# Adding the attention output bias to the first head's folded weights on PE, once, instead of to every tile on POOL

## The chip, the core and the metric

The kernel runs on one core of one Trainium2 chip. The metric is the device time of one execution in microseconds, given as the median of several runs. TensorE is written PE, VectorE DVE, ScalarE ACT, GpSimd POOL and the queue that issues most of the transfers SP, as in the profile.

## What is computed

A cross-attention block followed by a mixture-of-experts block, both with a layer norm ahead of them and a residual sum behind them. `x` is 4 x 1024 x 256, the context 4 x 64 x 192; there are 16 heads of 64 columns and 64 keys.

```
def attention(x, context, Wq, Wk, Wv, Wo, bo):
    q = (x @ Wq)          # heads of 64
    k, v = context @ Wk, context @ Wv
    attn = softmax(q k^T * scale)          # over the 64 keys of a head
    return (attn v over all heads) @ Wo + bo
x = x + attention(layernorm(x), ctx, Wq, Wk, Wv, Wo, bo)
x = x + ffn(layernorm(x))    # shared expert, and the best 2 of 8 experts by a gate
```

## The kernel before

The 4096 rows of x are 32 tiles of 128 rows. The kernel has three stages one behind the other: a preparation, the attention over the 32 tiles, and the expert stage over 103 tiles (20 and 12 shared ones around 71 routed ones), with the routing arithmetic between the last two.

**Preparation.** For every batch b two matrices are folded: `A` (Wq with the keys, so that scores = xn A) and `U` (the values with Wo, so that output = prob U). `U[b, j]` has 128 rows, which are the 64 keys of head 2j and the 64 keys of head 2j+1, and 256 columns. Every operand is split into a high and a low part in the fp32r type, and a product is three matmuls (high by high, low by high, high by low), written by the helper `product` (line 1086, the matmul is line 1092). The order is fixed by the list `plan` (line 379): entries C, W, K, A and then, for j = 0 to 7, V (j+1) and two U entries (j, i), each of which makes two batches. V of number 0 stands ahead of the two last A entries, and V of number 1 ahead of the first U entry. A V entry is a product with 128 and one with 64 contraction rows (192 in all), so six matmuls; a U entry is twelve matmuls of 256 columns with 128 contraction rows. Each entry goes through three engines: PE fills one of eight PSUM banks, ACT copies it out as the high part (line 710, `leave`), DVE subtracts that to get the low part (lines 913 to 933). Weights pass through ACT too (`high`, line 718) and then POOL, which makes their low parts (line 579) and increments `pre_w_lo`; PE waits for that count ahead of each K, V and U entry. In the ACT program the weights for V and U number j+1 are converted at the start of the V entry j.

**The passage to attention.** Every engine waits until all of the preparation is through PE, ACT and DVE (`pre_pe`, `pre_act`, `pre_dve`, all at NPRE). POOL then writes some constants (lines 586 to 596). ACT also waits for `const_ok` at 6, which is a matter of the very start of the kernel, since POOL's first six constants include `yrow` set to zero (line 535, 128 x 1024). ACT later issues DMAs that write these zeros to the accumulators in DRAM (`zero_rows`, line 760).

**Attention.** It is software-pipelined by hand: in step s each engine handles tile s + 1, s, s - 1 and so on, in a fixed order. For a tile: POOL and ACT make the normalized rows `xn`; PE transposes them (line 1165); ACT and DVE make the high and low parts `xTh` and `xTl` (lines 685, 875); PE computes scores (twelve matmuls of 512 columns in L1092); DVE takes maxima (line 862), scales them (`nmax`, line 865), subtracts (line 867); ACT takes exponentials (lines 700, 704); DVE sums and inverts (lines 841, 844); POOL normalizes `prob` (line 566); PE transposes it (line 1175), and multiplies with U (24 matmuls of 256 columns) into bank 5; DVE adds `xres`, the tile of x (line 891), and computes statistics for the second layer norm. SP loads `xres` (line 424). POOL adds `bo_bc`, the bias spread over 128 partitions, to `xres` at line 572, behind its normalization of another tile, and DVE waits for `xb_ok` that this sets. In steps 3, 4 and 5 POOL also makes low parts of the shared expert's weights (lines 601, 603, 606) at the end of its step.

Of the kernel before, what the change touches and what calls it, by code (L numbers as in the profile page):

```python
# [5 lines left out]
F32 = mybir.dt.float32  # L6
# [20 lines left out]
def xattn_moe(nc, x, ctx, Wq, Wk, Wv, Wo, bo, gate_w, gate_b, w1, b1, w3, b3, w2, b2,  # L27
# [43 lines left out]
    with stack:  # L71
# [18 lines left out]
        vTh = sb("vTh", [P, 2, B, 2, NK], F32R, pre)  # L90
        vTl = sb("vTl", [P, 2, B, 2, NK], F32R, pre)
        pre.close()
        xrow = sb("xrow", [P, RING, D], F32)
# [31 lines left out]
        Ul = sb("Ul", [P, B, NJ, D], F32R, att)  # L125
        bo_bc = sb("bo_bc", [P, D], F32, att)

# [105 lines left out]
        wo_in = sem("wo_in")  # L233
        small_in = sem("small_in")
        sw_in = sem("sw_in")
        id_ok = sem("id_ok")
# [39 lines left out]
        O_ok = sem("O_ok")  # L276
        xb_ok = sem("xb_ok")
        x2_ok = sem("x2_ok")
# [128 lines left out]
        def _(sp):  # L407
# [26 lines left out]
            sp.dma_start(wo_raw[:, :, :], Wo.rearrange("(j p) d -> p j d", p=P)).then_inc(wo_in, 16)  # L434
            sp.dma_start(bo_bc[:, :], bo.rearrange("(a d) -> a d", a=1).to_broadcast([P, D])).then_inc(small_in, 16)
            sp.dma_start(gateb_bc[:, :], gate_b.rearrange("(a d) -> a d", a=1).to_broadcast([P, E])).then_inc(small_in, 16)
# [85 lines left out]
        def _(pool):  # L522
# [11 lines left out]
            pool.iota(slots[:, :, 0], pattern=[[0, NU]], base=T, channel_multiplier=1).then_inc(const_ok, 1)  # L534
            pool.memset(yrow[:, :, :], 0.0).then_inc(const_ok, 1)
            pool.wait_ge(const_ok, 6)
            pool.dma_start(slots_dram.rearrange("(p n) c -> p n c", p=P), slots[:, :, :]).then_inc(table_out, 16)
            def tile_step(s, par):
# [23 lines left out]
                if has(t, NT):  # L562
# [4 lines left out]
                                       ALU.mult).then_inc(norm_ok, 1)  # L567
                t = s - 3
                if has(t, NT):
                    p = (par + 1) % 2  # L570
                    wait(pool, xres_in[p], before(t) + 16)
                    pool.tensor_tensor(xres[:, p, :], xres[:, p, :], bo_bc[:, :], ALU.add).then_inc(xb_ok, 1)

            for s in (-1, 0):
                tile_step(s, s % 2)
            for c, (kind, j) in enumerate(w_plan):
                pool.wait_ge(pre_w_hi, c + 1)
                for low, raw, high in zip(*(w_pieces(kind, j, name) for name in ("low", "raw", "high"))):
                    last = pool.tensor_tensor(low, raw, f32(high), ALU.subtract)
                last.then_inc(pre_w_lo, 1)  # L580
            pool.wait_ge(small_in, 96)
            pool.wait_ge(pre_pe, NPRE)
            pool.wait_ge(pre_act, NPRE)
            pool.wait_ge(pre_dve, NPRE)

            pool.memset(ones[:, :], 1.0).then_inc(const_ok, 1)
            pool.memset(tri[:, :], 1.0).then_inc(const_ok, 1)
# [69 lines left out]
        def _(act):  # L657
# [63 lines left out]
            for c, (kind, j, i) in enumerate(plan):  # L721
# [18 lines left out]
                elif kind == "A":  # L740
# [3 lines left out]
                    last.then_inc(pre_act, 1)  # L744
                elif kind == "V":
                    high("V", j + 1)
                    high("O", j + 1)
                    if j == 0:
                        act.wait_ge(vT_zero, 2)
                    for half, r in halves:  # L750
                        last = leave(c, vTh[half, j % 2, :, r, :],
                                     ps[half, c % 8, 0:BK].rearrange("p (b n) -> p b n", b=B))
                    last.then_inc(pre_act, 1)
                else:
                    leave(c, Uh[:, 2 * i:2 * i + 2, j, :], bank.rearrange("p (b d) -> p b d", b=2)).then_inc(pre_act, 1)
            act.wait_ge(pre_pe, NPRE)
            act.wait_ge(pre_dve, NPRE)
            act.wait_ge(small_in, 96)
            def zero_rows(rows):
# [13 lines left out]

            act.wait_ge(const_ok, 6)
            steps(NT, 1, 6, begin_step, begun=0)
# [56 lines left out]
        def _(dve):  # L832
# [3 lines left out]
            def tile_step(s, par):  # L836
# [48 lines left out]
                if has(t, NT):  # L885
                    p = par
                    wait(dve, O_ok, t + 1)
                    wait(dve, xb_ok, t + 1)
                    wait(dve, x2_out[p], before(t))
# [141 lines left out]
            for k, mark in enumerate((first, second)):  # L1031
                link(dve.tensor_tensor(mA[:, :, :], mark[:, :, :], score[:, :, :], ALU.mult))
                link(dve.tensor_reduce(record[:, :, k, 1].bitcast(F32), mA[:, :, :], AX.X, ALU.add))
            dve.wait_ge(small_in, 96)
            unit_step(0, 0)
# [47 lines left out]
        def _(pe):  # L1083
            PARTS = ((0, 0), (1, 0), (0, 1))

            def product(out, stationary, moving, n):


                last = None
                for k in range(n):  # L1090
                    for i, (a, b) in enumerate(PARTS):
                        last = pe.matmul(out, stationary(k, a), moving(k, b), start=(k == 0 and i == 0),  # L1092
                                         stop=(k == n - 1 and i == len(PARTS) - 1))
                return last
# [3 lines left out]
            for c, (kind, j, i) in enumerate(plan):  # L1098
# [23 lines left out]
                else:  # L1122
                    pe.wait_ge(pre_w_lo, w_number["O", j] + 1)
                    pe.wait_ge(pre_dve, number["V", j, 0] + 1)
                    for b in range(2):
                        last = product(bank[:, b * D:(b + 1) * D],
                                       lambda _, part: (vTh, vTl)[part][:, j % 2, 2 * i + b, :, :].rearrange("p a n -> p (a n)"),
                                       lambda _, part: (woh, wol)[part][:, j, :], 1)
                last.then_inc(pre_pe, 1)
            pe.wait_ge(pre_act, NPRE)  # L1130
            pe.wait_ge(pre_dve, NPRE)
            pe.wait_ge(small_in, 96)

# [169 lines left out]
```

## Time and profile before

| What | us |
|---|---|
| median of 3 runs | 806.48 (805.17 to 807.34) |
| the profiled execution | 811.39 |
| its span, first to last instruction | 809.5 |
| preparation, from the span's start | 0 to about 62 |
| attention | about 62 to 319 |
| routing arithmetic, and the last piece of weight loading | about 319 to 430 |
| expert stage | about 330 to 809 |

The profiled execution is 4.9 us longer than the median, and 1.9 us of it lies outside its span. The rows that follow are of its span. A timeline row gives start and duration in us, then engine, line, operation and tiles, and how many instructions it merges; "idle before" is the time that the engine stood still ahead of it, with what released it. A matmul's duration includes its pipeline depth, so that the distance between starts, and not the duration, is what a matmul adds to a stream of them.

### The profile page before, as it was taken

How to read it: one execution, taken by the hardware profiler on the slowest of the kernel's cores; microseconds unless marked ns; L12 is line 12 of the kernel's file. 1: busy time of each engine (PE TensorE's matmuls, PEld its weight loads, DVE VectorE, ACT ScalarE, POOL GpSimd, SP SyncE). 2: the span in 40 equal slices, each digit the busy share in tenths (PEclk: the TensorE clock that was granted, in tenths of full speed). 3: DMA queues.
4: the chain of work that ended last, by engine and by line, in shares of the span. 5: the costliest groups of instructions: out<-in, count | busy, mean ns of one | idle time of the engine just before them, and what ended most of it. 6: DMA issues, size and time to landing. Idle time of an engine off the chain costs nothing.

```text
span 809.5 us, 16280 instructions
## 1 busy us (share of the span) xinstructions
PE 675.1 (83%) x4635; PEld 633.8 (78%) x4636; DVE 535.4 (66%) x1053; ACT 396.9 (49%) x1287; POOL 423.1 (52%) x532
## 2 busy tenths in 40 slices
PE   3996899999999996603007888999999999999995
PEld 2785799999999985602007878999999999999994
DVE  3884888888888874810008888666666666666678
ACT  3995777787778772301007322343444434434432
POOL 4353866556556643377750120667667777676300
PEclk9997999999999999765558999999999999999998
DMA  9202333222222212990002321344444444445595
GB/s 214 80 1 104 129 126 88 77 66 79 66 75 71 66 56 85 296 335 11 1 4 82 106 80 53 60 79 72 72 71 72 77 69 73 73 83 109 88 370 227
DMA packets 65005, 79.96 MB, mean 99 GB/s; under 512 B 11337, under 2 KB 57906, under 8 KB 64946
## 3 DMA queue, kind: packets, MB, share of 16 engines
q1 hardware_dynamic: 47618, 55.81, 22.7%
q0 software_dynamic: 15744, 18.84, 14.7%
q10 hardware_dynamic: 1584, 4.59, 1.5%
q8 instruction: 30, 0.49, 0.2%
q14 instruction: 29, 0.24, 0.1%
HBM read 49.97 MB, written 29.24 MB: 98 GB/s over the span
## 4 chain that ended last, share of the span: by engine, by line
PE 74%; another core or an unknown queue 9%; DVE 8%; issue 3%; DMA 3%; ACT 2%; POOL 1%; SPq 0%; ACTq 0%; DVEq 0%; POOLq 0%
PE ps L1092 62%; PE ps L1247 4%; PE ps L1175 3%; PE ps L1239 2%; PE ps L1152 1%; DMA wq_sb<-in_L_xattn_Wq 1%; DMA xrow<-xn_scratch,slots 1%; DVE w13l L992 1%; DVE uv L969 1%; PE ps L1194 1%; PE ps L1165 1%; DVE hTl L956 1%; DVE hmax L862 0%; DVE w2l L995 0%
## 5 line engine op out<-in xcount | busy, mean ns | idle before, releaser
L641 POOL DMA_INDIRECT acc_scratch<-yrow,slots x71 | 111.5, 1570 | 87.6 <-ACT yrow L802 84.0
L634 POOL DMA_INDIRECT xrow<-xn_scratch,slots x71 | 70.8, 997 | 74.3 <-PE ps L1239 54.5
L802 ACT ACTIVATE yrow<-ps,slots 128x256 f32<-128x256 f32 x71 | 33.7, 474 | 148.1 <-PE ps L1092 148.1
L812 ACT ACTIVATE uxTh<-ps 128x256 fp32r<-128x256 f32 x103 | 38.9, 378 | 133.7 <-remote 71.9
L1092 PE MATMUL ps<-w13h,uxTh 128*128 x284 | 97.5, 343 | 0.0
L1092 PE MATMUL ps<-ws2h,hTh 128*128 128x256 f32 x96 | 29.4, 306 | 78.9 <-DVE hTl L956 55.0
L969 DVE TENSOR_TENSOR uv<-ps,b 128x704 f32<-128x704 f32 x71 | 63.3, 891 | 47.5 <-PE ps L1092 46.8
L1092 PE MATMUL ps<-w13l,uxTh 128*128 x284 | 91.7, 323 | 0.0
L1092 PE MATMUL ps<-w13h,uxTl 128*128 x284 | 91.3, 321 | 0.0
L1092 PEld LDWEIGHTS ps<-ws2h,hTh 128*128 128x128 f32 x96 | 19.0, 197 | 83.7 <-DVE hTl L956 59.5
L625 POOL DMA_INDIRECT slots_scratch<-record,slot x64 | 62.0, 969 | 33.8 <-issue 19.2
L700 ACT ACTIVATE prob<-ps,nmax 128x64 f32<-128x64 f32 x256 | 76.3, 338 | 3.1 <-DVE nmax L865 3.1
L951 DVE TENSOR_TENSOR uxTl<-ps,uxTh 128x256 fp32r<-128x256 f32 x103 | 43.6, 423 | 48.0 <-ACT uxTh L812 43.9
L1092 PE MATMUL ps<-Uh,pTh 128*128 128x256 f32 x256 | 74.9, 293 | 0.0
L1092 PE MATMUL ps<-Uh,pTl 128*128 128x256 f32 x256 | 72.3, 282 | 0.0
L1092 PE MATMUL ps<-Ul,pTh 128*128 128x256 f32 x256 | 71.9, 281 | 0.0
L566 POOL TENSOR_TENSOR prob<-prob,hinv 128x1024 f32<-128x1024 f32 x32 | 61.0, 1905 | 13.0 <-DVE hinv L844 13.0
L1092 PE MATMUL ps<-Ah,xTh 128*128 128x512 f32 x128 | 57.2, 447 | 8.1 <-DVE xTl L875 8.1
L1092 PE MATMUL ps<-w2h,hTh 128*128 x213 | 63.0, 296 | 0.0
L956 DVE TENSOR_TENSOR hTl<-ps,hTh 128x384 fp32r<-128x384 f32 x103 | 57.3, 556 | 7.5 <-issue 7.4
L969 DVE TENSOR_TENSOR uv<-ps,bs 128x704 f32<-128x704 f32 x32 | 28.4, 889 | 50.8 <-remote 31.8
L1092 PE MATMUL ps<-w2l,hTh 128*128 x213 | 60.1, 282 | 0.0
(206 smaller groups left out, 2250.7 us busy)
## 6 DMA issues: line engine op xcount, KB each, us to landing
sums<-acc_scratch SPq DMA_DIRECT2D x16, 512.0 KB, 10.0
w_raw<-in_L_ffn_w SPq DMA_DIRECT2D x16, 352.0 KB
xin<-in_x SPq DMA_DIRECT2D x32, 128.0 KB, 2.5
acc_scratch<-yrow ACTq DMA_DIRECT2D x8, 512.0 KB, 2.7
xres<-in_x SPq DMA_DIRECT2D x32, 128.0 KB, 2.4
acc_scratch<-x SPq DMA_DIRECT2D x32, 128.0 KB, 1.9
xn_scratch<-xn SPq DMA_DIRECT2D x32, 128.0 KB, 2.4
xrow<-xn_scratch SPq DMA_DIRECT2D x32, 128.0 KB
```

Of the source, the lines that this page charges most:

```text
L566: pool.tensor_tensor(heads, heads, hinv[:, p, :].unsqueeze(2).to_broadcast([P, HEADS, NK]), ALU.mult).then_inc(norm_ok, 1)
L625: pool.indirect_dma_start(slots_dram, bass.IndirectOffsetOnAxis(ap=slot[:, k, t:t + 1], axis=0), record[:, t, k, :], None).then_inc(scat_o ...
L634: pool.indirect_dma_start(xrow[:, m, :], None, xn2_dram, bass.IndirectOffsetOnAxis(ap=slots[:, u, 0:1], axis=0)).then_inc(gather_in[m], 16)
L641: pool.indirect_dma_start(acc_dram[u % 2], bass.IndirectOffsetOnAxis(ap=slots[:, u, 0:1], axis=0), yrow[:, m % YRING, :], None, compute_op ...
L700: act.activation(prob[:, p, h * NK:(h + 1) * NK], ps[:, s_bank(p) + h // 8, h % 8 * NK:(h % 8 + 1) * NK], ACT.Exp, bias=nmax[:, p, h - HS: ...
L802: act.activation(yrow[:, y, :], ps[:, 6 + m % 2, 0:D], ACT.Copy, scale=slots[:, bass.ds(u, 1), 1].bitcast(F32)).then_inc(y_ok, 1)
L812: act.activation(uxTh[:, p, :], ps[:, 0, 0:D], ACT.Copy).then_inc(uxTh_ok, 1)
L951: dve.tensor_tensor(uxTl[:, p, :], ps[:, 0, 0:D], f32(uxTh[:, p, :]), ALU.subtract).then_inc(uxTl_ok, 1)
L956: dve.tensor_tensor(hTl[:, :], ps[:, 5, 0:H3], f32(hTh[:, :]), ALU.subtract).then_inc(hTl_ok, 1)
L969: dve.tensor_tensor(uv[:, :, :], ps[:, 1 + 2 * p:3 + 2 * p, 0:H], bias, ALU.add).then_inc(bias_ok, 1)
L1092: last = pe.matmul(out, stationary(k, a), moving(k, b), start=(k == 0 and i == 0), stop=(k == n - 1 and i == len(PARTS) - 1))
L1247: last = pe.transpose(ps[:, 5, k * P:(k + 1) * P], hid[:, p, k * P:(k + 1) * P], ident[:, :])
```

## The change

The bias is no longer spread over 128 partitions but loaded as one row (`bo_row`, 1 x 256), split by ACT and POOL into `boh` and `bol`. Since the probabilities of a head sum to one, adding the bias to each of the 64 rows of U that belong to head 0 adds it once to each row of the output. So the four U products with j = 0 (one for each batch) are not closed after their three matmuls; two more with one contraction row follow, whose stationary operand `head0` is a row with ones in its first 64 of 128 columns and whose moving operands are `boh` and `bol`. POOL's addition at line 572, `bo_bc` and `xb_ok` go; DVE waits for the transfer of `xres` itself.

The five small buffers lie where `yrow` lies. So POOL can set `yrow` to zero only after the preparation: the memset is moved from the start of the kernel to the head of POOL's constants behind the preparation, and ACT, which waited for `const_ok` ahead of its first attention step, waits there for `zero_ok`, which the moved memset sets. `small_in` counts one transfer less.

```diff
@@ sync
-            sp.dma_start(bo_bc[:, :], bo.rearrange("(a d) -> a d", a=1).to_broadcast([P, D])).then_inc(small_in, 16)
+            sp.dma_start(bo_row[0:1, :], bo.rearrange("(a d) -> a d", a=1)).then_inc(bo_in, 16)
@@ gpsimd
-            pool.memset(yrow[:, :, :], 0.0).then_inc(const_ok, 1)
+            pool.memset(head0_raw[0:1, :], 0.0).then_inc(const_ok, 1)
             pool.wait_ge(const_ok, 6)
+            pool.memset(head0_raw[0:1, 0:NK], 1.0).then_inc(head0_ok, 1)
...
-                t = s - 3
-                if has(t, NT):
-                    p = (par + 1) % 2
-                    wait(pool, xres_in[p], before(t) + 16)
-                    pool.tensor_tensor(xres[:, p, :], xres[:, p, :], bo_bc[:, :], ALU.add).then_inc(xb_ok, 1)
...
             for c, (kind, j) in enumerate(w_plan):
+                if (kind, j) == ("V", 1):
+                    pool.wait_ge(bo_hi, 1)
+                    pool.tensor_tensor(bol[0:1, :], bo_row[0:1, :], f32(boh[0:1, :]), ALU.subtract).then_inc(bo_lo, 1)
                 pool.wait_ge(pre_w_hi, c + 1)
...
+            pool.memset(yrow[:, :, :], 0.0).then_inc(zero_ok, 1)
             pool.memset(ones[:, :], 1.0).then_inc(const_ok, 1)
@@ scalar
                 elif kind == "V":
+                    if j == 0:
+                        act.wait_ge(bo_in, 16)
+                        act.wait_ge(head0_ok, 1)
+                        act.activation(head0[0:1, :], head0_raw[0:1, :], ACT.Copy)
+                        act.activation(boh[0:1, :], bo_row[0:1, :], ACT.Copy).then_inc(bo_hi, 1)
                     high("V", j + 1)
                     high("O", j + 1)
...
-            act.wait_ge(const_ok, 6)
+            act.wait_ge(zero_ok, 1)
             steps(NT, 1, 6, begin_step, begun=0)
@@ vector
                     wait(dve, O_ok, t + 1)
-                    wait(dve, xb_ok, t + 1)
+                    wait(dve, xres_in[p], before(t) + 16)
@@ tensor
-            def product(out, stationary, moving, n):
+            def product(out, stationary, moving, n, more=False):
...
-                                         stop=(k == n - 1 and i == len(PARTS) - 1))
+                                         stop=(k == n - 1 and i == len(PARTS) - 1 and not more))
...
-                                       lambda _, part: (woh, wol)[part][:, j, :], 1)
+                                       lambda _, part: (woh, wol)[part][:, j, :], 1, more=j == 0)
+                        if j == 0:
+                            pe.wait_ge(bo_lo, 1)
+                            pe.matmul(bank[:, b * D:(b + 1) * D], head0[0:1, :], boh[0:1, :], start=False, stop=False)
+                            last = pe.matmul(bank[:, b * D:(b + 1) * D], head0[0:1, :], bol[0:1, :], start=False, stop=True)
```

## Rows read from the trace of the kernel before

**Rows 1.** The page's first part: busy time, share and instructions of each engine.
```profile
PE 675.1 (83%) x4635; PEld 633.8 (78%) x4636; DVE 535.4 (66%) x1053; ACT 396.9 (49%) x1287; POOL 423.1 (52%) x532
```

**Rows 2.** Stretches: busy time of PE, PEld, DVE, ACT, POOL; PE clock, DMA, GB/s.
```profile
38.00:61.70 23.70, 22.24 (x152) 19.25 (x151) 20.70 (x42) 21.60 (x62) 11.47 (x22) 1.00 0.00 1
...
61.70:90.00 28.30, 19.97 (x76) 15.61 (x77) 16.04 (x33) 16.99 (x66) 12.44 (x25) 0.82 0.31 107
...
119.00:200.00 81.00, 81.00 (x570) 74.84 (x570) 66.97 (x155) 62.54 (x253) 49.24 (x88) 1.00 0.27 78
```

**Rows 3.** Waits of PE from 0 to 170 us: total, times, longest.
```profile
PE ps L1092 <- DVE xTl L875: 8.1, 4, 2.7
...
PE ps L1165 <- ACT Uh L710: 1.5, 1, 1.5
```

**Rows 4.** Timeline of PE in a V entry of the preparation and the U entry behind it.
```profile
46.08 0.28 PE L1092 MATMUL ps<-ctxTl,wvh 128*128 128x256 f32 x1
46.29 0.38 PE L1092 MATMUL ps<-ctxTh,wvh 64*128 64x256 f32 x1
46.52 0.28 PE L1092 MATMUL ps<-ctxTh,wvl 64*128 64x256 f32 x1
46.63 0.28 PE L1092 MATMUL ps<-ctxTl,wvh 64*128 64x256 f32 x1
46.84 0.38 PE L1092 MATMUL ps<-woh,vTh 128*128 128x256 f32 x1
47.06 0.28 PE L1092 MATMUL ps<-woh,vTl 128*128 128x256 f32 x1
```

**Rows 5.** Timelines of ACT, POOL and PE where V number 1's weights are made.
```profile
39.14 0.51 ACT L718 ACTIVATE wvh<-wv_raw 128x128 fp32r<-128x128 f32 x2
39.54 0.42 ACT L718 ACTIVATE woh<-wo_raw 128x256 fp32r<-128x256 f32 x1
39.84 0.77 ACT L710 ACTIVATE vTh<-ps 64x256 fp32r<-64x256 f32 x2
...
39.72 0.88 POOL L579 TENSOR_TENSOR wvl<-wv_raw,wvh 128x128 fp32r<-128x128 f32 x2 [1.26 <-ACT wvh L718]
40.56 0.73 POOL L579 TENSOR_TENSOR wol<-wo_raw,woh 128x256 fp32r<-128x256 f32 x1
...
40.76 0.30 PE L1092 MATMUL ps<-ctxTh,wvh 128*128 128x256 f32 x1
```

**Rows 6.** The old bias transfer: issue duration in ns and start, time to landing.
```profile
L435 SPq DMA_DIRECT2D bo_bc<-in_L_xattn_bo x1: 6462/6462/6462, 5.7 to 5.7; - x1
...
DMA to landing us min/median/max: 14.3/14.3/14.3
```

**Rows 7.** Timeline: the memset of yrow, and the passage to attention.
```profile
3.27 0.94 POOL L535 MEMSET yrow<- 128x1024 f32 x1
...
61.92 0.60 ACT L678 ACTIVATE xn<-xin,nm,rs 128x256 f32<-128x256 f32 x1 [0.81 <-DVE Ul L932]
61.98 0.20 POOL L586 MEMSET ones<- 128x128 bf16 x1 [5.75 <-DVE Ul L932]
...
62.43 0.36 ACT L685 ACTIVATE xTh<-ps 128x256 fp32r<-128x256 f32 x1
```

**Rows 8.** The chain that ended last: scores of the first and the fourth tile.
```profile
63.30 4.63 PE ps L1092 x12
...
85.81 3.02 PE ps L1092 x12
```

**Rows 9.** POOL and DVE in the ramp; nmax (L865) over all tiles (min/median/max ns).
```profile
82.45 0.72 POOL L572 TENSOR_TENSOR xres<-xres,bo_bc 128x256 f32<-128x256 f32 x1
83.14 1.67 POOL L601 TENSOR_TENSOR ws13l<-ws,ws13h 128x704 fp32r<-128x704 f32 x1
...
83.36 1.47 DVE L865 TENSOR_SCALAR nmax<-hmax 128x8 f32<-128x8 f32 x1
...
L865 DVE TENSOR_SCALAR nmax<-hmax x32: 171/255/1473, 69.2 to 297.1; 128x8 f32<-128x8 f32 x32
```

More of the change, by code:

```diff
@@ L91, in xattn_moe @@
         vTl = sb("vTl", [P, 2, B, 2, NK], F32R, pre)
+        bo_row = sb("bo_row", [P, D], F32, pre)
+        boh = sb("boh", [P, D], F32R, pre)
+        bol = sb("bol", [P, D], F32R, pre)
+        head0_raw = sb("head0_raw", [P, P], F32, pre)
+        head0 = sb("head0", [P, P], F32R, pre)
         pre.close()
@@ L125, in xattn_moe @@
         Ul = sb("Ul", [P, B, NJ, D], F32R, att)
-        bo_bc = sb("bo_bc", [P, D], F32, att)
         xin = sb("xin", [P, 2, D], F32, att)
@@ L234, in xattn_moe @@
         small_in = sem("small_in")
+        bo_in = sem("bo_in")
+        bo_hi = sem("bo_hi")
+        bo_lo = sem("bo_lo")
+        head0_ok = sem("head0_ok")
+        zero_ok = sem("zero_ok")
         sw_in = sem("sw_in")
@@ L276, in xattn_moe @@
         O_ok = sem("O_ok")
-        xb_ok = sem("xb_ok")
         x2_ok = sem("x2_ok")
@@ L580, in _ @@
                 last.then_inc(pre_w_lo, 1)
-            pool.wait_ge(small_in, 96)
+            pool.wait_ge(small_in, 80)
             pool.wait_ge(pre_pe, NPRE)
@@ L757, in _ @@
             act.wait_ge(pre_dve, NPRE)
-            act.wait_ge(small_in, 96)
+            act.wait_ge(small_in, 80)
             def zero_rows(rows):
@@ L1033, in _ @@
                 link(dve.tensor_reduce(record[:, :, k, 1].bitcast(F32), mA[:, :, :], AX.X, ALU.add))
-            dve.wait_ge(small_in, 96)
+            dve.wait_ge(small_in, 80)
             unit_step(0, 0)
@@ L1131, in _ @@
             pe.wait_ge(pre_dve, NPRE)
-            pe.wait_ge(small_in, 96)
+            pe.wait_ge(small_in, 80)
             def tile_step(s, par):
```

## The prediction

> **What bounds the kernel now.** Start with the busy shares: PE is the busiest engine, POOL is busy for half of the span [rows 1]. That says nothing yet of what a microsecond of POOL is worth, so read the stretches [rows 2]. From 119 to 200 us, in the steady part of attention, PE is busy for 81.00 of 81.00 us at full clock, while POOL is busy for 49.24: PE is the bound and has no gap that a shorter POOL could close. In the second half of the preparation (38 to 61.7 us) PE is busy for 22.24 of 23.70 us, also at full clock, and ACT is close behind with 21.60. From 61.7 to 90 us, the ramp of the attention pipeline, PE is busy for only 19.97 of 28.30 us and its mean clock is 0.82: here a chain through all engines sets the pace. The waits of PE say which: four waits for `xTl` make 8.1 us, and 1.5 us passed between preparation and attention [rows 3]. So I read three places: the preparation, where PE is the bound; the passage; and the ramp. The change touches each.
>
> **Removed: 32 additions on POOL.** One takes 0.72 us [rows 9], 23 us in all. In the steady part they lie beside a PE without a gap, and are worth nothing. What hides them is PE's own stream; DVE, the reader of `xres`, waits for the U product behind it. The one place where such an addition stands on the chain is in the ramp: in step 3 it runs from 82.45, the 704-column subtraction for `ws13l` follows it at 83.14 and ends at 84.81, and DVE's `nmax`, started at 83.36, ends only at 84.83, 1.47 us long where its shortest is 0.17 [rows 9]. A DVE instruction of this kind evidently waits until the POOL instruction in progress is through. Behind it in DVE's order comes the `xTl` for which PE waits until 85.81 [rows 3, 8]. Without the addition the subtraction starts and ends 0.69 us sooner (83.14 less 82.45), and DVE and PE with it: a gain of 0.69. Steps 4 and 5 have the same pattern, but PE has work by then, so nothing.
>
> By the Trainium skill (the page SBUF — State Buffer, on what contends on the engine side) a GpSimd instruction and a VectorE instruction that uses two ports exclude each other for their whole length. The row agrees with that: `nmax` ends 0.02 us after the subtraction.
>
> **Added to PE.** Eight matmuls of 256 columns. Their distance within a stream is 0.12 us (46.52 to 46.63) [rows 4], so 8 times 0.118 gives 0.94. But they have one contraction row, and their neighbours 128. The trace has no such matmul; the nearest are those of 64 rows. The first of them starts 0.21 after its predecessor and its successor 0.23 after it; on the way back the distances are 0.21 and 0.22 (46.08, 46.29, 46.52; 46.63, 46.84, 47.06) [rows 4]. Against 0.118 that is 0.09, 0.11, 0.09 and 0.10: one excursion to fewer rows and back costs 0.4 us. The change makes four excursions, one for each batch: 1.6 us. Bounds: nothing if one row costs no switch (0), and twice the excursion if a narrower one costs more (3.2). I take 1.6, the only row that shows a change of rows. PE is the bound there, so this counts in full: 2.5 us.
>
> The Trainium skill (TensorEngine Tiling (Array Packing), key properties) states that a change of tiling mode drains the engine, which would put a price on each change as the rows do; the matmul page (TensorE: Matmul & The Clock Gate, why this matters for your kernels) has a small-row matmul as long as a full one, which taken alone gives the sum without the excursions. That case is a rival below.
>
> **Added to ACT and POOL in the preparation.** ACT copies `head0` (128 columns) and `boh` (256) ahead of the weights of V number 1. By starts, two copies of 128 columns take 0.40 (39.14 to 39.54) and one of 256 takes 0.30 (39.54 to 39.84) [rows 5]: 0.20 and 0.30, 0.5 together. So `boh` starts at 39.34 and ends about 39.75, and the V weights are high at 40.15 in place of 39.65. POOL starts 0.07 behind ACT; its 256-column subtraction is 0.73, at 39.82 to 40.55, and then the two subtractions for V take 0.88, to 41.4 in place of 40.60. PE took up V number 1 at 40.76 [rows 5], only 0.16 behind POOL's end, so it now waits until about 41.5: 0.7 us of stall, on the bound. The bounds are 0.3 (if the small copies cost half of it, with the subtraction of one row shorter) and 0.9. Behind it nothing more is late: the U products wait for `bo_lo` at 40.55, which is past; PE is now behind ACT by more than before, so later weights are in time. The stall and the 2.5 us arrive together at the end of the preparation, because ACT's last copies wait for PE, not the other way round.
>
> The transfer is one row in place of 128 KB. The old one was issued at 5.7 and landed 14.3 us later, about 20 us [rows 6]; ACT needs the row at 39.1. Nothing waits; SP's queue behind it only gets shorter, and what it loads there is used in attention. Two tiny memsets replace a 0.94 us one at POOL's start, where transfers of the weights are what PE waits for: nothing.
>
> **Moved: the memset of yrow.** It takes 0.94 us [rows 7]. POOL can begin it at 61.98, where it now begins `ones`. ACT waits for it before its first attention step: with 0.07 for the semaphore it starts at 62.99 in place of 61.92. Queued behind that wait are `xn` of tile 1 and then `xTh` of tile 0 (62.43), which DVE and PE wait for with the first scores at 63.30 [rows 7, 8]. Nothing covers it: 1.07 us. POOL's constants and its first statistics are late by 0.94 too, but ACT's use of them had room of its own behind the scores of tile 0.
>
> **Sum.** Preparation 0.94 + 1.6 + 0.7 = 3.2; passage 1.07; ramp -0.69: together +3.6 us. The profiled execution has 811.39, so the change would make it 815.0; on the median, 806.48 + 3.6 = 810.1, which is 0.45% slower. About 0.3%, 2.4 us, is what a measurement here can tell from no change.
>
> **Rivals.**
> *The rows cost no switch.* Then PE gets 0.94 and not 2.5: +2.0, 808.5, inside the limit. For it: one row is not 64, and I have one pattern only. Against it: that pattern repeats in each V entry.
> *The clock.* Scores of a tile in the ramp took 4.63 us where the fourth took 3.02 [rows 8], and the mean clock of the ramp was 0.82 [rows 2], so most of the first three groups ran at the lower of the two levels, 1.2 GHz; PE had stood idle ahead of each. The change makes the idle time ahead of the first group a microsecond longer and puts a stall into the preparation. If another group falls to the lower level, that costs 1.6 (4.63 less 3.02), and the result is 811.7.
> *On the other side: the ramp recovers its clock.* If the shift and the shorter gap in step 3 let the groups run at the upper level, each gives back 1.6. From the third group on the sum turns negative: 3.6 - 4.8 = -1.2, 805.3; with no cost for the switches, -2.8, which alone would be measurably faster (803.7). Two groups give 806.9. Against it: the gaps ahead of the first three groups become no shorter.
> *The relief counts after all.* `nmax` has a median of 0.255 where its shortest is 0.171 [rows 9], so POOL's instructions hold it up in most tiles, by 0.08 times 32, 2.7 us. If DVE paced the steady part, the net would be +0.9, 807.4. Against it: PE busy for 81.00 of 81.00 us.
> *The change does not do what it says.* If the new zeroing lay under other work, +2.5, 809.0. I see no such cover.
>
> **How the numbers follow.** The forecast, with its sizes about right: 0.55, 808.9 to 811.0. No switch cost: 0.15. Clock worse: 0.12. Clock better by one or more groups: 0.10, of which 0.03 is measurably faster. The relief: 0.03. The zeroing hidden: 0.05. The range that leaves out some 0.2, half of the clock cases and the ends of the switch's price: 807.2 to 812.0. Slower by over 0.3% (above 808.9) is 0.67: the forecast 0.52, the worse clock 0.12, and 0.03 of the hidden zeroing. Within 0.3% is 0.30, faster 0.03.
>
> **What would show it.** In the profile after: the eight matmuls with starts 0.2 apart at their edges, not 0.12; PE idle for 0.7 ahead of V number 1, released by POOL; a `yrow` memset of 0.94 between the last `Ul` and ACT's first `xn`, and first scores some 4.3 us later than 63.30; `nmax` of step 3 ending 0.69 sooner against the scores ahead of it; a steady step unchanged. It would be wrong if the four U products take 0.12 per matmul throughout, if PE waits somewhere new in the steady part, or if the clock in the ramp differs from 0.82.

## The result, and the profile after

The changed kernel takes 813.87 us (median of 7, 809.54 to 815.85) where the kernel before, measured beside it, takes 805.77 (805.01 to 807.97): a ratio of 1.0093, 95% interval 1.0069 to 1.0118. Measured a second time, beside the kernel before again (a1, below), it was 1.0085 (1.0070 to 1.0100). The change costs 7 to 8 us. The forecast was 3.6, with a range that ended at 812.0.

The profiled execution took 814.34, its span is 812.6. The page of the changed kernel, clock and shares:

```profile
PE 683.1 (84%) x4643; PEld 639.2 (79%) x4644; DVE 533.4 (66%) x1053; ACT 397.8 (49%) x1289; POOL 402.2 (50%) x503
...
PEclk9987899999999999675557999999999999999998
```

Two things differ from [rows 1] and its page: POOL lost 21 us of work, and the clock row begins 99878 where that of the kernel before begins 99979. The 7 in the fourth slice is the passage to attention in both. New are the 8 in the third slice, 41 to 61 us from the start, which is the preparation, and the 8 in the fifth, at the scores of tiles 2 and 3. PE is busy for 8 us more, although only eight small matmuls were added.

The first profile of the kernel before is not a typical one. The weights for Wq landed late in it: PE took up the first weight product at 14.62 us. In a second profile of the same kernel (b1, below) that is 11.53, and 11.67 in the changed kernel. In the other seventeen profiles of this document it lies between 11.50 and 12.36. So the two first profiles, 811.39 and 814.34, are only 3 apart, and stages are compared here by their own lengths, not by the time from the start.

Timeline of PE around the first U products of the changed kernel (L1144 and L1145 are the new matmuls, L1105 is the line of `product`):

```profile
37.81 0.36 PE L1105 MATMUL ps<-ctxTh,wvh 128*128 128x256 f32 x1 [0.56 <-issue]
...
39.23 0.28 PE L1105 MATMUL ps<-wol,vTh 128*128 128x256 f32 x1
39.44 0.38 PE L1144 MATMUL ps<-boh,head 1*128 1x256 f32 x1
39.66 0.28 PE L1145 MATMUL ps<-bol,head 1*128 1x256 f32 x1
39.87 0.38 PE L1105 MATMUL ps<-woh,vTh 128*128 128x256 f32 x1
40.09 0.28 PE L1105 MATMUL ps<-woh,vTl 128*128 128x256 f32 x1
...
45.43 0.41 PE L1105 MATMUL ps<-woh,vTl 128*128 128x256 f32 x1
45.65 0.41 PE L1105 MATMUL ps<-wol,vTh 128*128 128x256 f32 x1
45.86 0.41 PE L1105 MATMUL ps<-woh,vTh 128*128 128x256 f32 x1
```

The first row is V number 1 with the stall ahead of it. The profile names no releaser for it (`issue`), but POOL's rows show it: the split of the bias runs ahead of the weights of V number 1, and PE starts 0.10 behind the end of those (36.85 + 0.86), as it started 0.16 behind it before.

```profile
36.15 0.73 POOL L583 TENSOR_TENSOR bol<-bo_row,boh 1x256 fp32r<-1x256 f32 x1 [1.36 <-ACT boh L758]
36.85 0.86 POOL L586 TENSOR_TENSOR wvl<-wv_raw,wvh 128x128 fp32r<-128x128 f32 x2
```

The next rows answer to [rows 4]: the distances at the edges of an excursion are 0.21, 0.22, 0.21 and 0.22, as with 64 rows to 0.01. The last three are ordinary matmuls of 128 rows that start 0.21 apart where they start 0.12 apart in the kernel before. The stretches say why (length, then PE, PEld, DVE, ACT and POOL busy, then PE's clock, DMA share, GB/s):

```profile
38.00:42.40 4.40, 4.40 (x24) 3.15 (x23) 3.28 (x8) 2.59 (x9) 1.96 (x4) 0.98 0.00 0
42.40:49.00 6.60, 6.60 (x26) 5.65 (x26) 2.58 (x5) 3.63 (x11) 1.55 (x3) 0.50 0.00 0
49.00:62.90 13.90, 13.66 (x99) 12.13 (x98) 11.00 (x21) 12.27 (x32) 6.29 (x12) 1.00 0.00 1
```

For 6.6 us PE ran at 1.2 GHz. The fall came behind three of the four pairs of one-row matmuls; the fourth pair, at 42.45, is already at the lower clock. There are 26 matmuls in the 6.6 us where the second profile of the kernel before has 48 at full clock:

```profile
42.40:49.00 6.60, 6.60 (x48) 5.79 (x48) 5.89 (x12) 6.53 (x20) 3.94 (x8) 1.00 0.00 0
```

The passage to attention of the changed kernel, from its timeline:

```profile
64.50 0.96 POOL L593 MEMSET yrow<- 128x1024 f32 x1 [5.77 <-DVE Ul L945]
65.64 0.60 ACT L686 ACTIVATE xn<-xin,nm,rs 128x256 f32<-128x256 f32 x1 [2.02 <-POOL yrow L593]
66.15 0.36 ACT L693 ACTIVATE xTh<-ps 128x256 fp32r<-128x256 f32 x1
```

Beside [rows 7] one sees ACT standing idle for the memset, where it stood idle for the last `Ul` before. From the end of the last `Ul` (64.35) to the first scores (67.02) 2.67 us pass, before 1.46 (61.84 to 63.30). The scores of the first four tiles, as the chain has them, answer to [rows 8]:

```profile
67.02 5.50 PE ps L1105 x12
...
74.96 4.34 PE ps L1105 x12
...
81.73 4.30 PE ps L1105 x12
...
89.40 4.59 PE ps L1105 x12
```

The fourth group takes 4.59 where it took 3.02: in this profile one more group fell to the lower clock, as the prediction's rival has it. In the second profile of the changed kernel (a1) it takes 3.04. Over the 28.3 us from the last `Ul` on, the mean clock is 0.71 here and 0.82 in the kernel before.

The steady part is as it was, with POOL lighter; this row answers to the last of [rows 2]:

```profile
119.00:200.00 81.00, 81.00 (x570) 74.84 (x570) 65.99 (x155) 62.41 (x252) 42.10 (x77) 1.00 0.28 84
```

### The profile page after: what moved, and what is told of

The parts are those of the page before. It is cut to its first block, busy times and chain, and to the rows that moved or that the text cites. A ratio compares the mean times of both kernels' runs of the same rounds, so it can differ in the third digit from the quotient of the medians.

```text
span 812.6 us, 16270 instructions
## 1 busy us (share of the span) xinstructions
PE 683.1 (84%) x4643; PEld 639.2 (79%) x4644; DVE 533.4 (66%) x1053; ACT 397.8 (49%) x1289; POOL 402.2 (50%) x503
## 3 DMA queue, kind: packets, MB, share of 16 engines
q10 hardware_dynamic: 1584, 4.59, 1.5%
## 4 chain that ended last, share of the span: by engine, by line
PE 74%; another core or an unknown queue 8%; DVE 8%; issue 4%; ACT 2%; DMA 2%; POOL 1%; SPq 0%; DVEq 0%; ACTq 0%; POOLq 0%
PE ps L1105 61%; PE ps L1264 4%; PE ps L1192 3%; PE ps L1256 2%; PE ps L1169 2%; DVE w13l L1005 1%; DVE uv L982 1%; DMA wq_sb<-in_L_xattn_Wq 1%; PE ps L1211 1%; PE ps L1182 1%; DVE hTl L969 1%; DMA xrow<-xn_scratch,slots 1%; DVE w2l L1008 1%; ACT w13h L798 0%
## 5 line engine op out<-in xcount | busy, mean ns | idle before, releaser
L1105 PE MATMUL ps<-w13h,uxTh 128*128 x284 | 97.5, 343 | 0.0
L1105 PE MATMUL ps<-ws2h,hTh 128*128 128x256 f32 x96 | 29.5, 307 | 76.9 <-DVE hTl L969 67.1
L1105 PE MATMUL ps<-w13l,uxTh 128*128 x284 | 91.7, 323 | 0.0
L1105 PE MATMUL ps<-w13h,uxTl 128*128 x284 | 91.3, 321 | 0.0
L1105 PEld LDWEIGHTS ps<-ws2h,hTh 128*128 128x128 f32 x96 | 19.0, 198 | 82.0 <-DVE hTl L969 71.9
L964 DVE TENSOR_TENSOR uxTl<-ps,uxTh 128x256 fp32r<-128x256 f32 x103 | 43.6, 423 | 50.8 <-ACT uxTh L825 42.0
L1105 PE MATMUL ps<-Uh,pTh 128*128 128x256 f32 x256 | 74.9, 293 | 0.0
L1105 PE MATMUL ps<-Uh,pTl 128*128 128x256 f32 x256 | 72.3, 282 | 0.0
L1105 PE MATMUL ps<-Ul,pTh 128*128 128x256 f32 x256 | 71.9, 281 | 0.0
L1105 PE MATMUL ps<-Ah,xTh 128*128 128x512 f32 x128 | 58.0, 453 | 8.1 <-DVE xTl L888 8.1
L1105 PE MATMUL ps<-w2h,hTh 128*128 x213 | 63.0, 296 | 0.0
L1105 PE MATMUL ps<-w2l,hTh 128*128 x213 | 60.1, 282 | 0.0
L1105 PE MATMUL ps<-w2h,hTl 128*128 x213 | 60.0, 281 | 0.0
```

Of the source, the lines that this page charges most:

```text
L964: dve.tensor_tensor(uxTl[:, p, :], ps[:, 0, 0:D], f32(uxTh[:, p, :]), ALU.subtract).then_inc(uxTl_ok, 1)
```

## The experiments

Ratios are to the kernel before, measured beside each kernel. The times of single executions of one kernel spread over 2 to 11 us, so each profile is one draw. The diffs are cut to the lines that carry the experiment; what only follows from them is left out, and "..." marks a cut. "U products" is the time from the first U matmul to the end of the last one.

One correction: the description ahead of the prediction gives a U entry twelve matmuls. It has six (two batches of three); the two U entries of one j have twelve. The count of added matmuls, eight, is not touched.

**b1: the kernel before, profiled again.** No edit.

> The kernel before, unchanged, profiled a second time, because its first profiled execution (811.4) lies 5.6 above its median (805.8). If the late landing of the weights for Wq in that execution (PE took up the first weight product at 14.6 us, in the changed kernel at 11.7) is chance, this profile has it near 11.7 and the whole time near 806; if it belongs to the kernel before (its 128 KB bias transfer, its long memset), it is near 14.6 again. Either way the clock is 1.0 from 38 us to the end of the preparation, and the ratio of times is 1.000 within 0.002.

Ratio 0.999 (0.9979 to 1.0002), 806.78. The late landing was chance, though the profiled execution, 809.28, lies above its median too:

```profile
11.19 0.69 PE L1111 MATMUL ps<-ident,wq_sb 128*128 128x128 f32 x2 [4.51 <-DMA wq_sb<-in_L_xattn_Wq]
11.53 0.56 PE L1092 MATMUL ps<-ctxTh,wkh 128*128 128x256 f32 x1
```

U products take 18.74 in it, 18.71 in the first profile.

**a1: the changed kernel, profiled again.** No edit.

> The changed kernel, unchanged, profiled a second time. Theory R (one-row matmuls lower the clock): from the first U product to the last it takes 24 us or more again (24.1 in its first profile, 18.7 in both of the kernel before, 19.6 with full rows), with matmul starts 0.21 apart in a part of it; passage 2.67 us again; time near 814. Rival C (the fall was chance): 21.3 us, 2.54 more than before, with the clock at 1.0.

814.50, ratio 1.0085 (1.0070 to 1.0100); the profiled execution took 817.43. The clock fell again, later and for longer, from about 44.3 to 54.3; the row is of the inner part:

```profile
45.50:53.60 8.10, 8.10 (x36) 7.43 (x34) 3.77 (x8) 4.29 (x11) 2.86 (x6) 0.50 0.01 2
```

U products: 24.10 in the first profile, 25.61 here.

**e1: bias matmuls with 128 rows.**

```diff
-            pe.matmul(bank[...], head0[0:1, :], boh[0:1, :], ...)
+            pe.matmul(bank[...], head0[:, :], boh[:, :], ...)      # bol the same
...
-            sp.dma_start(bo_row[0:1, :], bo.rearrange("(a d) -> a d", a=1))
+            sp.dma_start(bo_row[:, :], bo.rearrange("(a d) -> a d", a=1).to_broadcast([P, D]))
```

> The changed kernel with bias matmuls of 128 contraction rows: the bias is spread over 128 partitions, and head0 has zeros in rows 1 to 127. The eight matmuls, the additions on ACT and POOL, the stall and the moved memset stay. Theory R (the one-row matmuls make the excursions and are also why the clock fell to 1.2 GHz from 42.4 to 49 us in the preparation): starts 0.12 apart throughout, clock 1.0 in the preparation, 4 to 5 us faster than the changed kernel, near 809. Rival S (the clock fell because PE stood still for 0.56 us ahead of V number 1): only the excursions go, 1.6 us, and the clock falls as before, near 812. Rival C (the fall is chance): it is seen in some executions with either kernel, and the medians differ by 1.6.

Ratio 1.0036 (1.0023 to 1.0048): more than half of the loss is gone, 4 to 5 us. The eight matmuls fit into the stream without an edge, and the U products take 19.62, which is 0.9 over the kernel before:

```profile
42.21 0.28 PE L1105 MATMUL ps<-wol,vTh 128*128 128x256 f32 x1
42.32 0.28 PE L1144 MATMUL ps<-boh,head 128*128 128x256 f32 x1
42.44 0.28 PE L1145 MATMUL ps<-bol,head 128*128 128x256 f32 x1
42.56 0.28 PE L1105 MATMUL ps<-woh,vTh 128*128 128x256 f32 x1
```

The stall is still there (V number 0 to V number 1 takes 3.24, before 2.49) and the clock in the preparation is 1.0. So the stall alone does not lower it.

**e2: no bias matmuls.**

```diff
-            pe.matmul(bank[...], head0[0:1, :], boh[0:1, :], start=False, stop=False)
-            last = pe.matmul(bank[...], head0[0:1, :], bol[0:1, :], start=False, stop=True)
```

> The changed kernel without its eight bias matmuls, so that the bias is left out of the output; ACT's copies, POOL's split, the stall that they cause and the moved memset stay. Theory R: clock 1.0 in the preparation; 0.9 less than e1, near 808. Rival S: the stall is still there, so the clock falls, near 811.

Ratio 1.0033 (1.0014 to 1.0051), U products 18.70, clock 1.0 with the stall in place (3.22). The bias is missing from this kernel's output. Rival S has fallen. But 2.7 us are left (1.1 to 4.1 by the interval) where the sum of stall, passage and relief is 1.2; that pointed to the passage without proving it.

**e3: ACT waits for the zeros behind its first step.**

```diff
-            act.wait_ge(zero_ok, 1)
             steps(NT, 1, 6, begin_step, begun=0)
@@ begin_step, behind tile_step
+                if s == 0:
+                    act.wait_ge(zero_ok, 1)
```

> The changed kernel with ACT's wait for the zeroed yrow put behind its first attention step, ahead of the first transfer that reads it. If the wait held up the first scores, they start 1.1 to 1.2 us sooner after the last subtraction of the preparation, and the time falls by 1.1 (to near 812.7); what is queued there (xTh of tile 0) no longer waits. Rival: the constants that POOL makes behind the memset, or its statistics for tile 2, are late instead, and nothing is gained.

Ratio 1.0070 (1.0051 to 1.0089); the changed kernel has 1.0093 and 1.0085, so 1.2 to 1.9 us, within the intervals. Its passage is 1.46 (67.15 to 68.61), that of the kernel before, with the memset beside ACT's work. The mechanism is as expected; one measurement of this size does not settle its price. The clock fell in its preparation too; U products take 25.61.

**e9: the kernel before with the memset moved.**

```diff
-            pool.memset(yrow[:, :, :], 0.0).then_inc(const_ok, 1)
+            pool.memset(yrow[:, 0, 0:1], 0.0).then_inc(const_ok, 1)
...
+            pool.memset(yrow[:, :, :], 0.0).then_inc(zero_ok, 1)
             pool.memset(ones[:, :], 1.0).then_inc(const_ok, 1)
...
-            act.wait_ge(const_ok, 6)
+            act.wait_ge(zero_ok, 1)
```

> The kernel before with one edit of the change alone: yrow is set to zero behind the preparation and ACT waits for it ahead of its first step. Passage 2.67 us in place of 1.46, so 1.2 slower, ratio 1.0015. If the longer standstill of PE also costs clock in the ramp, as e2 hints (2.7 measured where 1.2 was the sum), it is 2 to 3, ratio 1.003.

Ratio 1.0030 (1.0012 to 1.0048), 2.4 us, twice the 1.2 by which the passage is longer; but the interval, 1.0 to 3.9 us, holds 1.2 as well. Its chain:

```profile
61.08 0.96 POOL yrow L587
...
63.60 5.49 PE ps L1094 x12
```

The scores of tile 0 take 5.49, at the lower clock from end to end. Over all eighteen profiles, the first group takes 3.03 to 4.62 us in the nine with a passage of 1.46 (before, b1, e3, e4, e6, e10 to e13) and 4.23 to 5.49 in the nine with 2.67 (both of the changed kernel, e1, e2, e5, e7, e8, e9, e14), from the first start to the last end: means 4.2 and 5.0. So the longer standstill of PE goes with about 0.8 us more in the group behind it, beside its own 1.2. Counted from the last `Ul` to the end of the sixth group, the means are 40.0 and 41.8, so 1.8 in all; but single profiles lie between 38.6 and 43.9, and the shortest of the eighteen, e2, is one with the longer passage. That the standstill costs clock is likely; its price is not settled.

**e4: the kernel before without POOL's additions.** The bias is left out.

```diff
...
-                    pool.tensor_tensor(xres[:, p, :], xres[:, p, :], bo_bc[:, :], ALU.add).then_inc(xb_ok, 1)
...
-                    wait(dve, xb_ok, t + 1)
+                    wait(dve, xres_in[p], before(t) + 16)
```

> The kernel before with POOL's 32 bias additions taken out alone (the bias is left out of the output). Theory: they are worth what the third nmax of the ramp is shorter, 0.7 us (1.47 to about 0.8), so 0.1% faster at most; the steady step stays at 7.41. Rival: nmax is held up in most tiles, 0.08 each, and DVE counts after all: 2.7 us, 0.3%.

Ratio 0.9991 (0.9980 to 1.0002): 0.7 us, not told apart from nothing, and the rival's 0.3% lies outside the interval. The bias is missing from the output here, so this is all that the change could have gained, whatever the new way to add the bias.

**e5 and e14: the split of the bias made early.** ACT's two copies and POOL's subtraction stand at W entry 5 and ahead of the K weights number 7.

```diff
 elif kind == "W":
     high("K", j + 1)
+    if j == 5:
+        act.wait_ge(bo_in, 16)
+        act.wait_ge(head0_ok, 1)
+        act.activation(head0[0:1, :], head0_raw[0:1, :], ACT.Copy)
+        act.activation(boh[0:1, :], bo_row[0:1, :], ACT.Copy).then_inc(bo_hi, 1)
...
@@ gpsimd
-    if (kind, j) == ("V", 1):
+    if (kind, j) == ("K", 7):
```

> The changed kernel with the bias split (ACT's two copies, POOL's subtraction) moved ahead, to the W entry 5, where POOL stands idle for 1.8 us; one-row matmuls and the moved memset stay. Theory: PE's stall of 0.56 to 0.7 ahead of V number 1 goes (first product to first product of V number 0 and 1 is 2.49 apart again, not 3.2) and the clock still falls behind the one-row matmuls: 0.7 faster than the changed kernel. Rival S: the clock fell for the stall, so it stays at 1.0 and the time falls by 3.5 or more.

> The kernel of e5 once more. If the fall of the clock moves with the place of the narrow matmuls in time, this profile shows U products of 24 to 28 us with the clock at 0.5 to 0.8 for two or three stretches, and a time near 815; the mean of both measurements is what counts. If it measures near 812 to 813, e5's 816.5 was a matter of few executions.

Neither theory came out. The stall is gone in both profiles (2.57 and 2.59 from V to V), and so is the fall of the clock: U products 21.18 and 21.17, the price of excursions and streams alone (2.5 over 18.7). Yet the ratios are 1.0118 (1.0096 to 1.0140) and 1.0134 (1.0111 to 1.0156), worse than the changed kernel. The profiled executions are the fastest of their kernels: in e14 747.35 at a mean clock of 0.971, while the four others took 755.25 to 758.50 at 0.958 to 0.964. An estimate from these means: 0.961 of 755 us is half clock for 59 us, 0.971 of 746 for 43 (twice the missing share); half of the 16 between them is 8 us, and 8 to 11 are missing. So the clock was lower for longer in those, but where it fell the records do not tell. Why a kernel without the stall loses more by it than one with the stall stays open.

**e6: three edits together.** e1, e3 and e5 in one kernel.

> The changed kernel with three edits: bias matmuls of 128 rows, the split at W entry 5, ACT's wait for zero_ok behind its first step. If the costs are the ones named and add up, what is left is eight matmuls (0.94) less the relief in the ramp (0.5 to 0.7): within 0.5 us of the kernel before, ratio 1.000 to 1.001. If something else of the change costs time (the shorter POOL lets something collide, the transfer of xres waited for by DVE), it shows here as what is left above 1.001.

Ratio 0.9998 (0.9988 to 1.0009). The loss is gone. What remains of the change, the lighter POOL, the changed wait of DVE and eight full matmuls, weighs nothing together, and nothing else of it costs a time that shows (the interval is -1.0 to +0.7 us). It is no faster than the kernel before.

**e10: e6 with one-row matmuls.**

```diff
-            pe.matmul(bank[...], head0[:, :], boh[:, :], ...)
+            pe.matmul(bank[...], head0[0:1, :], boh[0:1, :], ...)  # bol the same
```

> As e6 (split moved ahead, ACT's wait put behind its first step), but with the one-row matmuls of the changed kernel. It differs from e6 in the rows alone, which nothing else now touches. Theory R: the excursions give 1.6 and the clock, which fell in three of four profiles with one-row matmuls for 2.9 to 4.4 us of cost, gives 2 to 4: 3.6 to 6 above e6, ratio to the kernel before 1.004 to 1.007. If the clock needs the stall as well, it is 1.6 above e6, ratio 1.002.

Ratio 1.0054 (1.0038 to 1.0070): 4.5 us over e6 by the rows alone. Its profile shows no fall in the preparation (U products 21.19, clock 1.0), yet the profiled execution took 810.57. Five of the six executions, this one among them, have a mean clock of 0.928 to 0.930. So here the mean clock does not tell one execution from another. In this profile the lower clock shows behind the passage (from 62 to 95 us 0.84, in e6's profile 0.90); where the other executions have theirs the records do not tell.

**e7: bias matmuls with 64 rows.**

```diff
-            pe.matmul(bank[...], head0[:, :], boh[:, :], ...)
+            pe.matmul(bank[...], head0[0:64, :], boh[0:64, :], ...)  # bol the same
```

> As e1, but the bias matmuls read 64 rows of head0 and of the bias in place of 128. The four excursions are back, at 0.4 each, and the number of rows that work is 64 and not 1. If the clock falls for the few rows, it stays at 1.0 here, U products take 21.2 in all and the time is 1.6 above e1 (ratio 1.0055). If the gaps of the excursions are what lowers it, the clock falls as with one row, and the ratio is 1.008 to 1.01 as for the changed kernel.

Ratio 1.0058 (1.0042 to 1.0074), e1 plus 1.8 us. U products 21.18: the same excursions as with one row, and no fall.

**e8: two excursions in place of four.** `fold(b)` is the product of batch b, three full matmuls.

```diff
...
+                    if j == 0:
+                        fold(0, more=True)
+                        pe.wait_ge(bo_lo, 1)
+                        for b in range(2):
+                            for k, part in enumerate((boh, bol)):
+                                pe.matmul(bank[:, b * D:(b + 1) * D], head0[0:1, :], part[0:1, :],
+                                          start=(b == 1 and k == 0), stop=(b == 0 and k == 1))
+                        last = fold(1, first=False)
...
```

> The changed kernel with the bias matmuls of a U entry side by side: the first batch has its three full matmuls and then the two one-row ones, the second batch the one-row ones first. Eight one-row matmuls as before, but two excursions in place of four. Excursions: 0.8 us less, U products 23.3 or less in all. If the number of one-row matmuls lowers the clock, it still falls; if the excursions do, it falls less often, and the median is 2 or more below the changed kernel's.

Ratio 1.0023 (1.0012 to 1.0034). The median, 810.5, is 3 to 4 below the changed kernel's, and only 0.8 of it is the excursions. Here the profiled execution, 818.2, is the slowest of 13 by 6.7, and in it the clock fell (U products 24.86):

```profile
45.00:54.00 9.00, 9.00 (x38) 8.10 (x38) 4.31 (x8) 5.30 (x14) 3.10 (x6) 0.50 0.00 0
```

By its times the fall has become rare (the other twelve took 807.95 to 811.5), though only one profile was taken. The number of one-row matmuls is the same, so the number alone does not decide; how they are spread counts. The ratio is even below that of e1, which has neither excursions nor a fall, and 1.9 us (1.0 to 2.7) is less than the sum of the costs without any fall. That stays open.

**e11, e12, e13: sixteen bias matmuls with 1, 64 and 128 rows.** On e6; the added ones multiply a row of zeros, and `rows` stands for the number.

```diff
-            pe.matmul(bank[...], head0[:, :], boh[:, :], start=False, stop=False)
+            for part in (boh, none, none):
+                pe.matmul(bank[...], head0[0:rows, :], part[0:rows, :], start=False, stop=False)
```

> As e10, but each bias pair of one-row matmuls is followed by two more one-row matmuls that add a row of zeros: 16 in place of 8, in the same four excursions. Their streams cost 0.94 more. If few rows lower the clock, it falls in nearly every execution and for longer: 3 us or more above e10 beside the 0.94, ratio 1.009 or more. If the gaps of the excursions do it, the clock falls as in e10: ratio 1.0065.

> As e11, with 64 rows in all 16. If few rows lower the clock, it does not fall (64 rows did not lower it in e7): e6 plus 1.6 and 0.94, ratio 1.003. If the gaps do it, the same time as e11.

> As e11, with 128 rows in all 16, so no excursions: e6 plus 0.94, ratio 1.001, clock 1.0 in the preparation. It is the baseline for e11 and e12 in both theories.

These ran on a chip on which the kernel before takes 747.0. Ratios: 1.0081 (1.0065 to 1.0098), 1.0017 (1.0001 to 1.0032), 0.9997 (0.9979 to 1.0015), so 6.1, 1.3 and -0.2 us. U products: 25.08, 22.08, 20.56. Between 64 and 128 rows lie 1.52, four excursions of 0.38. Between 1 and 64 rows, with the same count, the same edges and the same order, lie 3.00 in the profile and 4.8 in the ratio. All six executions of e11 have a mean clock of 0.960 to 0.963, all twelve of e12 one of 0.967 to 0.975. So it is clock, in the rows of e11 and then e12:

```profile
44.00:51.00 7.00, 7.00 (x30) 5.97 (x29) 2.92 (x5) 4.17 (x12) 2.04 (x5) 0.55 0.00 0
```

```profile
44.00:51.00 7.00, 7.00 (x52) 6.32 (x52) 5.21 (x10) 6.78 (x21) 4.32 (x9) 1.00 0.00 0
```

In e11 PE is at 0.50 from 43.6 to 50.2. The theory of the gaps has fallen as the sole cause, since gaps with 64 rows do nothing to the clock. In all, the clock fell in the preparation in 5 of the 8 profiles with one-row matmuls and in none of the 10 without.

## Why the prediction was wrong

The direction was right and the size was not: 7 to 8 us where 3.6 was forecast. The step that failed is "PE is the bound there, so this counts in full: 2.5 us", which priced the added matmuls at full clock and left PE's clock in the preparation out of the sum. The U products took 5.4 and 6.9 us more in the two profiles (24.10 and 25.61 against 18.71), and of that 2.9 and 4.4 are the lower clock. By the steps of the prediction:

**The streams and the excursions, 2.5.** Right at full clock. In the four profiles where eight narrow matmuls in four excursions met full clock (e5, e7, e10, e14), the U products take 21.17 to 21.19 against 18.7: 2.48. The row with 64 rows that was the nearest one gave the price of a single row exactly, and the rival of no switch cost is dead.

**The stall, 0.7.** Right: V to V took 3.20 in place of 2.49, and without the late split 2.57.

**The memset, 1.07.** The place was right, and 1.21 was measured: the memset starts 0.15 after the last `Ul` (64.35), takes 0.96 and ACT starts 0.18 behind its end. The step that said "nothing covers it" holds. Missing from it was the clock behind it, some 0.8 by the profiles and 1.2 by e9, with the interval of e9 reaching down to nothing.

**The relief, -0.69.** Right. `nmax` of step 3 took 1.12 in the first profile after, 0.80 to 0.82 in e1, e3 and a1, against 1.47 to 1.49 in all three with the addition; e4 gives 0.7. Nothing came of it in the steady part.

**The sum** of the terms as measured is 2.48 + 0.71 + 1.21 - 0.7 = 3.7, and in this the forecast was right to 0.1. The rest, some 4 us, is clock. The sum has no term for it. Only a rival has one, with 0.12 and one group's worth, 1.6, and it looked for the cause in PE standing still: the longer gap ahead of the first scores and the stall. The first of these is small, if it is real; the stall did not lower the clock in e1, e2 and e7. The larger part, some 3 us, comes from the kind of matmul that was added, in a stretch where PE has work all the time. That the stage had clock 1.0 throughout was read as a state of affairs, and not as something that the added work could end.

For the changed kernel, e1 and e6 the accounts close. With rows of 128 (e1) the sum is 0.94 + 0.7 + 2.4 (passage with its clock, e9) - 0.7 = 3.3 and 2.9 was measured. For one row, 1.54 for the excursions and some 3 for the clock come on top: 7.5 to 7.9, and 6.9 to 7.5 was measured by the ratios. The 3 for the clock is 3.0 in e10 over e6 less the excursions, 2.2 to 2.8 in the changed kernel over e7, and 4.8 in e11 over e12. That it is lost in the preparation is seen in five profiles with one-row matmuls, not in that of e10. Taking the costs away (e6) leaves 0. The accounts do not close for e8, 2 us below the sum, and for e5 and e14, 2 to 3 above the changed kernel though they lack its stall.

**Chances.** 0.67 on slower was well placed. The range left out the two causes together: its upper end, 812.0, is about the forecast and one group of scores, and the loss of clock in the preparation was not among the cases at all.

The Trainium skill (TensorE: Matmul & The Clock Gate, what's actually happening) has the clock follow how busy PE has been, and names idle time as what lowers it. The runs add to that: in the stretch ahead of the fall (38 to 42.4) PE is busy in the records for 4.40 of 4.40 us, with matmuls of one row among the others, and it falls all the same; e11 beside e12 shows that it is the rows. The same page of the Trainium skill has a matmul of few rows as long as a full one (why this matters for your kernels). That holds for its own duration, 0.28 with one row as with 128, and leaves out the 0.4 us of each excursion. The Trainium skill (TensorEngine Tiling (Array Packing), key properties) states that a change of tiling mode drains the engine; the late starts at the edges fit that.

## What to carry to other kernels

A small piece of work moved off an idle engine onto the one that sets the pace costs its full price there, and 32 additions of 0.72 us less on POOL were worth 0.7. A bias row added by a matmul should have the contraction rows of its neighbours: padded with zeros to 128 rows each matmul cost 0.12 us here; with one row each pair cost an excursion of 0.4 us on top and often, in this dense stream, the clock of what followed. Before moving an initialization past a barrier, ask who waits first behind it: the wait belongs ahead of the first reader (here a transfer), not ahead of the stage.

## What the hardware showed that was not expected

- Full utilization in the records does not keep PE's clock. With eight one-row matmuls, or sixteen of them (e11), it fell to 1.2 GHz for 6.6 to 10.0 us in the preparation, in five of eight profiles; with 64 rows in the same places it did not.
- How the one-row matmuls are spread counts as well: side by side in two excursions (e8), the loss fell from 7 or 8 us to 1.9. Why e5 and e14 lose 9 to 10 us, and e8 less than its costs, stays open.
- Behind a standstill of PE that is longer by 1.2 us the first group of scores took 0.8 us more in the mean of nine profiles each. Whether the kernel's time grows by as much is not settled.
- A profile is one execution. For e5 and e14 the profiled one was the fastest of its kernel, and for e8 it was the only one far off; for e5 and e14 the mean clock listed with each timed execution was what told. For e8 and e10 it does not: in e8 0.927 stands beside 818.2 and beside 811.5.
- One chip ran the kernel before in 747.0 us, the others in 806 to 807.5. In its profiles PE's mean clock from 330 to 430 us is 0.93 to 0.94, in e5's on another chip 0.60; that stage was not studied.
